# Network passes of a graph kernel: GpSimd waits for landings at every second group of gathers, and SyncE loads two groups at a time

## The chip, the cores and the metric

The kernel runs on one core of a Trainium2 chip. The metric is device time in microseconds. In this document PE is TensorE, DVE is VectorE, ACT is ScalarE, POOL is GpSimd and SP is SyncE, which computes nothing here and issues plain DMAs.

## The reference, cut to what matters

Four graph layers follow each other over 6,250 nodes of 64 features and 206,250 directed edges (sorted by destination). The change touches the third, whose message function runs twice:

```python
def _propagate(h, edge_attr, edge_index, We, be, Wl):
    x_i = h[edge_index[0]]
    x_j = h[edge_index[1]]
    x_edge = jnp.concatenate([x_i, x_j, edge_attr], axis=-1)
    x_edge = _mlp1(x_edge, We, be)              # silu(x @ W + b)
    x_edge = edge_attr @ Wl * x_edge
    x_p = _seg_mean(x_edge, edge_index[0], h.shape[0])
    return x_p + h
```

Since `We` is applied to a concatenation, the kernel adds three products: one of the node that sums (looked up from SBUF by a one-hot matmul), one of the other node (gathered from a table `q_table` in HBM), and one of the edge (stored earlier in a record of the edge, `rec_src`).

## The kernel before, in words

Edges stand in buckets of destination nodes, 128 edges to a tile, and a group is 8 tiles (`U = 8`), so 1,024 edges. There are `NG = 216` groups, and each of the two network passes (`k = 0, 1`) walks through all of them. Loops run over 54 iterations of four groups (`n = 0..3`); most buffers have four slots (`gat4`, `pay4`, `lo_bc`, `ring_i`) or two (`oht`, `msg`, `onehot`). I write g for a group's number within a pass, g = 4i + n.

The order is written out by hand on each engine, and semaphores tie the engines:

- POOL, `node_rows` and `gathers` (lines 637 to 651): for group g it waits until the 8 index columns are there (`l_idx`), then until the gathers of group g-1 have landed (`landed[(n - 1) % 4]`, which is `l_gat`), and issues 8 indirect DMAs, each of which gathers 128 rows of 64 floats into `gat4[n]`. The second wait is left out only for the first group of all.
- SP, `load_edges` (lines 521 to 523): for group g two plain loads, 552 KB of edge records into `pay4[n]` and 256 KB of digit rows, spread over the partitions, into `lo_bc[n]`. `load_all_edges` issues those of group g as soon as the message and the one-hot rows of group g-4 are done and its slots are free.
- ACT, in the order of its program for group g: `distance(g+2)` (line 862, waits for the digit rows of g+2 to land), `onehot_rows(g+1)` (line 867), `silu(g)` (line 872).
- PE, for group g: `look_up(g+1)` (line 1173, 8 matmuls, needs the one-hot rows of g+1), then `sums(g)` (line 1183, 8 matmuls, needs the message of g).
- DVE, for group g: `node_part(g)` (line 1563), `onehot_columns(g+1)` (line 1550, two operations, needs `sums(g-1)`), `edge_part(g+1)` (line 1558, waits for the gathers and the records of g+1), `message(g)` (line 1568, needs `silu(g)`), `index(g+4)` (line 1545, which lets POOL begin group g+4), and the four chained additions of `gather_sums(g-1)` (line 1578).

Line 645 is shared with a third pass of gathers, over `h_table`, which the change leaves as it is. `hold` is a wait followed by an increment of a semaphore that nothing waits for.

Of the kernel before, what the change touches and what calls it, by code (L numbers as in the profile page):

```python
# [20 lines left out]
U = 8  # L21
# [15 lines left out]
NG = TT // U  # L37
OFF = 4
# [68 lines left out]
def build(nc, a, out):  # L107
    ctx = ExitStack()
    with ctx:
# [3 lines left out]
        def sem(name):  # L113
            return ctx.enter_context(nc.semaphore(name))
# [4 lines left out]
        q_table = [nc.dram_tensor(f"q_table{k}", (NP, D), F32).ap() for k in range(2)]  # L119
# [84 lines left out]
        excess, own, first, elsewhere, trash = [dup_i[:, n] for n in range(5)]  # L204
# [39 lines left out]
        gat4 = [gat_flat[:, n * U * D:(n + 1) * U * D].rearrange("p (u d) -> p u d", u=U) for n in range(4)]  # L244
# [120 lines left out]
        l_gat = [sem(f"l_gat{n}") for n in range(4)]  # L365
# [3 lines left out]
        l_oht = sem("l_oht")  # L369
# [5 lines left out]
        l_msg = sem("l_msg")  # L375
# [35 lines left out]
        def hold(eng, s, value):  # L411

            eng.wait_ge(s, value)
            eng.sem_inc(s_passed, 1)
# [39 lines left out]
        def _(sp):  # L454
# [66 lines left out]
            def load_edges(k, i, n):  # L521
                sp.dma_start(pay4[n], rec[:, bass.ds(i * (4 * U) + n * U, U), :]).then_inc(l_pay[n], 16)
                sp.dma_start(lo_bc[n], lo_rows[bass.ds(i * 4 + n, 1), :].to_broadcast([P, U * P])).then_inc(l_lo[n], 16)

            def load_all_edges(k):
                if k:
                    sp.wait_ge(f_res, NCH * 4)
                    sp.wait_ge(l_msg, NG + OFF)
                    sp.wait_ge(l_oht, NG + OFF)
                for n in range(4):  # L530
                    load_edges(k, 0, n)
                with sp.Fori(1, NG // 4) as i:
                    for n in range(4):
                        sp.wait_ge(l_msg, i * 4 + (k * NG + n - 3 + OFF))
                        sp.wait_ge(l_oht, i * 4 + (k * NG + n - 3 + OFF))
                        load_edges(k, i, n)

            for k in range(2):
                store_table(EV_PQ + k, q_table[k], acc[:])
                load_all_edges(k)  # L540
# [29 lines left out]
        def _(pool):  # L570
# [66 lines left out]
                pool.wait_ge(d_scat[q], EI * 16 * U)  # L637


            def gathers(table, rows, landed, i, n, before, first):  # L640

                if not first:
                    hold(pool, landed[(n - 1) % len(landed)], i * (16 * U) + before)
                for u in range(U):
                    nc.gpsimd.indirect_dma_start(  # L645
                        rows[n][:, u, :], None, table,
                        bass.IndirectOffsetOnAxis(ring_i[:, n, u:u + 1], 0)).then_inc(landed[n], 16)

            def node_rows(k, i, n, first=False):
                hold(pool, l_idx, i * 4 + (k * NG + n + 1))  # L650
                gathers(q_table[k], gat4, l_gat, i, n, (k * (NG // 4) + (n > 0)) * 16 * U, first)

            for k in range(2):
                pool.wait_ge(d_table, 16 * (1 + k))
                for n in range(4):
                    node_rows(k, 0, n, first=k == 0 and n == 0)
                with pool.Fori(1, NG // 4) as i:
                    for n in range(4):
                        node_rows(k, i, n)

            def score_rows(i, n, first=False):
                hold(pool, t_idx, nth(i, n))
                gathers(h_table, gat8, t_gat, i, n, (n > 0) * 16 * U, first)
# [10 lines left out]
        def _(act):  # L674
# [104 lines left out]
            def node_copies(tr, ev, dst, rows):  # L779
                for c, (_, n) in enumerate(CHUNKS):  # L780
                    act.wait_ge(n_tr, NCH * tr + c + 1)
                    if c >= 2:
                        act.wait_ge(n_mm, NCH * ev + c - 1)
                    act.copy(dst[0:rows, c % 2, 0:n * P], bank[c % 2][0:rows, 0:n * P]).then_inc(n_cp, 1)
# [145 lines left out]
        def _(pe):  # L930
# [53 lines left out]
            def project(ev, lhs, weights, width, tr=None, chunk=None):  # L984


                if chunk:
                    chunk(0)
                for c, (_, n) in enumerate(CHUNKS):
                    if chunk:  # L990
                        if c + 1 < NCH:
                            chunk(c + 1)
                        pe.wait_ge(n_cp, NCH * tr + c + 1)
                    if c >= 2:
                        pe.wait_ge(n_ev, NCH * ev + c - 1)
                    for j in range(n):
                        b, o = bank[2 + c % 2], j * width
                        if o + width > 512:
                            b, o = bank[4 + c % 2], 0
                        last = mm(b[:, o:o + width], lhs(c, j), weights(c) if callable(weights) else weights, start=True, stop=True)  # L1000
                    last.then_inc(n_mm, 1)
# [57 lines left out]
            def project_out(k):  # L1059
                for c, (_, n) in enumerate(CHUNKS):  # L1060
                    if c % 2 == 0:
                        pe.wait_ge(a_out, (k - 1) * (DUOS + 1) + c // 2 + 1)
                    if c >= 2:
                        pe.wait_ge(n_ev, NCH * k + c - 1)
                    for j in range(n):
                        last = mm(bank[2 + c % 2][:, j * D:(j + 1) * D], out_chunk(c, j), halves(w_conv[k], c % 2), start=True, stop=True)
                    last.then_inc(n_mm, 1)
# [798 lines left out]
```

## Time and profile before

| what | value |
|---|---|
| median of 3 runs | 16204.83 us (16196.27 to 16240.02) |
| the profiled execution | 16222.93 us, span 16221.2 us |
| POOL busy | 9525.9 us (59%) |
| PE busy | 9592.5 us (59%) |
| DVE busy | 7215.4 us (44%) |
| network pass 0, gathers from first to last | 7210.7 to 10017.3 us |
| network pass 1, gathers from first to last | 10228.2 to 13035.1 us |

Busy time is the sum of the durations of an engine's instructions. A view of waits lists the idle time of an engine just before an instruction, together with what ended it; "issue" there is idle time in which the profile shows nothing that was waited for. In a timeline the number in brackets is that same idle time, and the name behind the arrow is what ended it. SPq rows are DMA issues of SP.

### The profile page before, as it was taken

To read this page: it belongs to the slowest core of one execution; us is meant where nothing else is said; L and a number is where in the kernel's file an instruction comes from. 1 tells how busy PE (TensorE), PEld (TensorE's weight loads), DVE (VectorE), ACT (ScalarE), POOL (GpSimd) and SP (SyncE) were. 2 spreads that over 40 slices of the span, in tenths; PEclk is the share of its full clock that TensorE was granted. 3 is DMA by queue.
4 is the path that set the end of the run, shared out by engine and by line. 5 is a ranking of instruction groups with operands and counts; after the bars stand their busy time and mean duration, and the time that the engine had idled before them with its cause. 6 is when DMAs were issued, how large, how long until landed. Compare 5 with 4: busy or idle time off the path is not lost.

```text
span 16221.2 us, 180153 instructions
## 1 busy us (share of the span) xinstructions
PE 9592.5 (59%) x40895; PEld 6450.1 (40%) x40896; DVE 7215.4 (44%) x18628; ACT 3844.3 (24%) x8556; POOL 9525.9 (59%) x8465
## 2 busy tenths in 40 slices
PE   0466657766478878845555556655555545555555
PEld 0111122221133333335555554555555545555554
DVE  8876657777000000013333332333333357777776
ACT  0344444442011111112222222222222212222221
POOL 0378878888645434426666664566666645555553
PEclk9999999999688778865555555555555555555555
DMA  9922222222599989992222223222222344444444
GB/s 385 358 15 19 19 15 20 20 20 18 168 342 370 343 306 357 359 113 86 84 86 84 85 84 50 75 84 86 84 86 85 80 95 139 141 141 140 140 139 96
DMA packets 1483063, 2197.01 MB, mean 135 GB/s; under 512 B 882955, under 2 KB 926027, under 8 KB 1454669
## 3 DMA queue, kind: packets, MB, share of 16 engines
q1 hardware_dynamic: 907628, 1490.52, 28.2%
q0 software_dynamic: 453120, 343.50, 12.7%
q10 hardware_dynamic: 121698, 356.43, 6.0%
q8 instruction: 184, 3.01, 0.1%
q14 instruction: 433, 3.55, 0.1%
HBM read 1771.19 MB, written 419.98 MB: 135 GB/s over the span
## 4 chain that ended last, share of the span: by engine, by line
POOL 40%; DMA 22%; issue 21%; PE 8%; DVE 4%; another core or an unknown queue 3%; ACT 1%; POOLq 0%; SPq 0%; DVEq 0%; ACTq 0%
POOL gat L645 18%; POOL adj L613 12%; POOL arena L645 8%; DMA arena<-adj 8%; DMA gat<-q_table,ring_i 6%; DMA arena<-h_table,ring_i 5%; PE bank L1029 5%; DMA adj<-put_n,put_at 2%; POOL rec_src L599 1%; DVE arena L1356 1%; PE same L1161 1%; PE same L1000 1%; DVE arena L1358 1%; PE same L980 0%
## 5 line engine op out<-in xcount | busy, mean ns | idle before, releaser
L645 POOL DMA_INDIRECT gat<-q_table,ring_i x3456 | 3626.6, 1049 | 2405.7 <-DMA gat<-q_table,ring_i 1025.0
L613 POOL DMA_INDIRECT adj<-put_n,put_at x1632 | 2559.9, 1569 | 1265.3 <-DVE put_at L1440 638.1
L1183 PE MATMUL bank<-onehot_t,onehot 128*128 128x64 f32 x6912 | 1585.5, 424 | 2574.9 <-DVE acc L1578 1880.5
L1183 PEld LDWEIGHTS bank<-onehot_t,onehot 128*128 128x128 f32 x6912 | 1506.7, 330 | 2653.8 <-DVE acc L1578 1938.5
L599 POOL DMA_INDIRECT rec_src<-pay,ring_i x1632 | 1606.4, 984 | 1566.9 <-ACTq L743 1093.2
L645 POOL DMA_INDIRECT arena<-h_table,ring_i x1728 | 1729.4, 1001 | 1346.2 <-DMA arena<-h_table,ring_i 760.8
L1088 PE MATMUL same<-onehot 32*128 32x512 f16 x3264 | 1678.6, 615 | 620.0 <-DVE onehot L1411 389.3
L1029 PE MATMUL bank<-arena,hs 128*64 128x512 f32 x5880 | 1596.0, 707 | 508.2 <-DMA arena<-adj 506.9
L1419 DVE TENSOR_SCALAR_CACHE_REDUCE onehot<-same 128x128 bf16<-128x128 f32 (+3 forms) x1632 | 1233.0, 756 | 843.2 <-PE same L1090 675.9
L1173 PE MATMUL bank<-hs,arena 128*128 x6912 | 1564.0, 421 | 29.3 <-ACT arena L867 29.3
L1173 PEld LDWEIGHTS bank<-hs,arena 128*128 128x128 f32 x6912 | 1525.9, 333 | 29.8 <-issue 29.8
L1558 DVE TENSOR_TENSOR gat<-gat,arena 128x512 f32<-128x512 f32 x432 | 299.3, 693 | 2774.6 <-DMA gat<-q_table,ring_i 2774.6
L754 ACT ACTIVATE arena<-iota_lo,arena 128x128 bf16<-128x128 f32 x3264 | 996.5, 387 | 1110.4 <-PE bank L960 926.9
L872 ACT ACTIVATE onehot_t<-gat 128x512 f32<-128x512 f32 x432 | 272.7, 631 | 3865.7 <-DVE gat L1563 3858.1
L1029 PEld LDWEIGHTS bank<-arena,hs 128*64 128x64 f32 x5880 | 525.3, 163 | 1477.0 <-issue 1473.9
L1422 DVE TENSOR_SCALAR_CACHE_REDUCE onehot<-same 128x896 bf16<-128x896 f32 (+6 forms) x1428 | 979.8, 686 | 0.0
L739 ACT COPY pay<-bank 128x260 f32<-128x260 f32 x816 | 299.9, 377 | 2283.2 <-PE bank L953 2059.2
L1509 DVE TENSOR_TENSOR acc<-bank,gat 128x512 f32<-128x512 f32 x20 | 13.8, 692 | 1828.9 <-PE bank L1038 1476.9
L1550 DVE TENSOR_TENSOR onehot<-iota_lo,keep 128x512 f32<-128x512 f32 x864 | 559.0, 689 | 566.7 <-PE bank L1183 418.2
L1239 PE MATMUL bank<-hs,pay 128*128 128x4 f32 x1728 | 386.0, 355 | 642.4 <-DVE hs L1705 478.7
L1090 PEld LDWEIGHTS same<-later,ident 128*128 128x128 f16 x1632 | 172.4, 106 | 1364.3 <-issue 1364.3
L1239 PE MATMUL bank<-hs,onehot_t 128*128 128x4 f32 x1728 | 385.2, 355 | 557.0 <-DVE hs L1705 338.3
(277 smaller groups left out, 13003.2 us busy)
## 6 DMA issues: line engine op xcount, KB each, us to landing
arena<-adj SPq DMA_DIRECT2D x300, 2560.0 KB
arena<-rec_src SPq DMA_DIRECT2D x432, 552.0 KB
adj<-hs ACTq DMA_DIRECT2D x25, 6656.0 KB, 46.3
rec_src<-pay ACTq DMA_DIRECT2D x1, 119232.0 KB, 332.0
arena<-lo_row SPq DMA_DIRECT2D x432, 256.0 KB
hs<-b_row SPq DMA_DIRECT2D x108, 1024.0 KB
acc<-b_row SPq DMA_DIRECT2D x108, 1024.0 KB
gat<-q_table,ring_i POOLq DMA_INDIRECT x3456
```

What stands on the lines that cost most here:

```text
L599: nc.gpsimd.indirect_dma_start(rec_src, bass.IndirectOffsetOnAxis(ring_i[:, q, u:u + 1], 0), pay[:, q, u, :], None, bounds_check=SLOTS - 1 ...
L613: nc.gpsimd.indirect_dma_start(counts, bass.IndirectOffsetOnAxis(put_at[:, b // 3 % 4, c:c + 1], 0), put_n[:, b // 3 % 4, c:c + 1], None, ...
L645: nc.gpsimd.indirect_dma_start(rows[n][:, u, :], None, table, bass.IndirectOffsetOnAxis(ring_i[:, n, u:u + 1], 0)).then_inc(landed[n], 16)
L754: last = act.activation(bh_lo[:, q, u, :], iota_lo[:], ACT.Abs, bias=lo_f[key][:, bass.ds(column + u, 1)], scale=-1.0)
L1029: last = [mm(sums[n], hs[:, m, :], a_ring4[(g + n) % 4][:, cell, half * ND:(half + 1) * ND], start=m == 0, stop=False) for n in range(2)]
L1088: mm(bank[2 * (n % 2) + half], rows[:, t * P:(t + 1) * P], rows[:, half * 512:(half + 1) * 512], start=True, stop=half != t // 4)
L1173: last = mm(bank[4 + n % 2][:, u * D:(u + 1) * D], oht[n % 2][:, u * P:(u + 1) * P], hs_flat[:, bass.ds(his[u // 2] * D, D)], start=True, ...
L1183: last = mm(bank[6 + n % 2][:, u // 2 * D:(u // 2 + 1) * D], onehot[:, n % 2, u, :], msg[n % 2][:, u, :], start=u % 2 == 0, stop=u % 2 == 1)
L1239: last = mm(bank[6 + (n + 1) % 2][:, u * 4:(u + 1) * 4], oht_l3[(n + 1) % 2][:, u * P:(u + 1) * P], nt[(n + 1) % 4][:, :, u // 2 + 1], sta ...
L1419: last = v.tensor_scalar(out_[:, 0:(t + 1) * P], seen[:, 0:(t + 1) * P], THR, 0.0, ALU.max, ALU.add, accum_out=s_upto[r][:, c:c + 1])
L1422: last = v.tensor_scalar(out_[:, (t + 1) * P:W * P], seen[:, (t + 1) * P:W * P], THR, 0.0, ALU.max, ALU.add, accum_out=s_past[r][:, c:c + 1])
L1550: last = v.tensor_tensor(onehot[:, n % 2, u0:u0 + U // 2], iota_lo[:].unsqueeze(1).to_broadcast([P, U // 2, P]), wide(tabs[1][:, bass.ds(i ...
```

## The change

Two places are edited. POOL's `gathers` gets a parameter `burst`, and the network passes call it with 2: the wait for the landing of group g-1 is made only where n is 0 or 2. So POOL issues the 16 gathers of a pair of groups (e and e+1, with e even) with no wait for a landing between them. The wait for the indices stays at every group, and the third pass of gathers keeps `burst=1`. SP's loop now also goes in pairs: it waits until the gathers of e-1 have landed, and until the message and one-hot rows of e-3 are done, and then issues the four loads of e and e+1 together.

```diff
                 with sp.Fori(1, NG // 4) as i:
-                    for n in range(4):
-                        sp.wait_ge(l_msg, i * 4 + (k * NG + n - 3 + OFF))
-                        sp.wait_ge(l_oht, i * 4 + (k * NG + n - 3 + OFF))
+                    for n in range(0, 4, 2):
+                        hold(sp, l_gat[(n - 1) % 4], i * (16 * U) + (k * (NG // 4) + (n > 0)) * 16 * U)
+                        hold(sp, l_msg, i * 4 + (k * NG + n - 2 + OFF))
+                        hold(sp, l_oht, i * 4 + (k * NG + n - 2 + OFF))
                         load_edges(k, i, n)
+                        load_edges(k, i, n + 1)
...
-            def gathers(table, rows, landed, i, n, before, first):
+            def gathers(table, rows, landed, i, n, before, first, burst=1):
 
-                if not first:
+                if not first and n % burst == 0:
                     hold(pool, landed[(n - 1) % len(landed)], i * (16 * U) + before)
...
             def node_rows(k, i, n, first=False):
                 hold(pool, l_idx, i * 4 + (k * NG + n + 1))
-                gathers(q_table[k], gat4, l_gat, i, n, (k * (NG // 4) + (n > 0)) * 16 * U, first)
+                gathers(q_table[k], gat4, l_gat, i, n, (k * (NG // 4) + (n > 0)) * 16 * U, first, burst=2)
```

## Rows read from the trace of the kernel before

**Rows 1.** The page: span, and the chain that ended last, by engine and line

```profile
span 16221.2 us, 180153 instructions
...
POOL 40%; DMA 22%; issue 21%; PE 8%; DVE 4%; another core or an unknown queue 3%; ACT 1%; POOLq 0%; SPq 0%; DVEq 0%; ACTq 0%
POOL gat L645 18%; POOL adj L613 12%; POOL arena L645 8%; DMA arena<-adj 8%; DMA gat<-q_table,ring_i 6%; DMA arena<-h_table,ring_i 5%; PE bank L1029 5%; DMA adj<-put_n,put_at 2%; POOL rec_src L599 1%; DVE arena L1356 1%; PE same L1161 1%; PE same L1000 1%; DVE arena L1358 1%; PE same L980 0%
```

**Rows 2.** Busy time by stretch: the two network passes (clock, DMA share, GB/s last)

```profile
7210.00:10017.00 2807.00, 1523.00 (x6880) 1483.71 (x6880) 889.85 (x2140) 588.49 (x647) 1812.93 (x1728) 0.50 0.30 83
10228.00:13035.00 2807.00, 1523.00 (x6880) 1483.69 (x6880) 889.32 (x2140) 587.54 (x646) 1813.30 (x1728) 0.50 0.30 83
```

**Rows 3.** POOL's waits, whole run: us in total, times, longest

```profile
POOL gat L645 <- DMA gat<-q_table,ring_i: 1025.0, 429, 8.4
POOL gat L645 <- issue: 961.8, 3025, 2.2
```

**Rows 4.** Timeline of one group: start, us, engine, line, operation, idle before

```profile
8041.86 0.95 POOL L645 DMA_INDIRECT gat<-q_table,ring_i  x1 [0.30 <-issue]
8044.40 0.69 DVE L1558 TENSOR_TENSOR gat<-gat,arena 128x512 f32<-128x512 f32 x1 [6.16 <-DMA gat<-q_table,ring_i]
8045.01 0.69 DVE L1568 TENSOR_TENSOR onehot_t<-onehot_t,arena 128x512 f32<-128x512 f32 x1
8045.04 1.47 POOL L645 DMA_INDIRECT gat<-q_table,ring_i  x1 [2.23 <-DMA gat<-q_table,ring_i]
...
8045.87 0.33 SPq L522 DMA_DIRECT2D arena<-rec_src  x1
...
8045.96 3.67 PE L1183 MATMUL bank<-onehot_t,onehot 128*128 128x64 f32 x16 [5.75 <-DVE acc L1578]
...
8046.39 0.33 SPq L523 DMA_DIRECT2D arena<-lo_row  x1
...
8049.43 3.62 PE L1173 MATMUL bank<-hs,arena 128*128 x16
8049.83 1.29 DVE L1550 TENSOR_TENSOR onehot<-iota_lo,keep 128x512 f32<-128x512 f32 x2 [1.07 <-PE bank L1183]
8050.57 1.37 POOL L645 DMA_INDIRECT gat<-q_table,ring_i  x1 [0.30 <-issue]
8050.74 1.15 ACT L862 ACTIVATE arena<-arena,neg_p 128x1024 bf16<-128x1024 bf16 x1 [1.24 <-issue]
8051.80 1.04 ACT L867 ACTIVATE arena<-arena 128x1024 f32<-128x1024 bf16 x1
...
8057.92 1.47 POOL L645 DMA_INDIRECT gat<-q_table,ring_i  x1 [2.23 <-DMA gat<-q_table,ring_i]
```

**Rows 5.** POOL's timeline in an earlier stage: 16 scatters in a row

```profile
4501.67 0.97 POOL L599 DMA_INDIRECT rec_src<-pay,ring_i  x1 [4.69 <-ACTq L743]
...
4511.89 0.98 POOL L599 DMA_INDIRECT rec_src<-pay,ring_i  x1 [0.30 <-issue]
...
4520.85 0.97 POOL L599 DMA_INDIRECT rec_src<-pay,ring_i  x1 [0.30 <-issue]
```

**Rows 6.** Slices of 1 us after a load was issued (DMA share, GB/s last)

```profile
8034.00:8035.00 1.00, 1.00 (x7) 1.00 (x7) 0.58 (x3) 0.00 (x0) 0.95 (x1) 0.50 0.94 212
8035.00:8036.00 1.00, 1.00 (x7) 1.00 (x6) 0.46 (x1) 0.51 (x1) 0.73 (x1) 0.50 0.99 335
8036.00:8037.00 1.00, 1.00 (x6) 1.00 (x6) 0.06 (x1) 0.12 (x1) 0.69 (x2) 0.50 0.83 309
```

**Rows 7.** Groups of instructions, 7400 to 9600 us: busy us, mean ns, idle before

```profile
L645 POOL DMA_INDIRECT gat<-q_table,ring_i x1368 | 1437.1, 1051 | 763.7 <-DMA gat<-q_table,ring_i 383.2 <-issue 380.4
...
L1558 DVE TENSOR_TENSOR gat<-gat,arena 128x512 f32<-128x512 f32 x171 | 118.5, 693 | 1064.4 <-DMA gat<-q_table,ring_i 1064.4
...
L872 ACT ACTIVATE onehot_t<-gat 128x512 f32<-128x512 f32 x171 | 108.0, 631 | 1506.1 <-DVE gat L1563 1506.1
```

## The prediction, made before the change was run

> **What bounds the kernel now.** I read the chain that ended last first, because only what lies on it can move the end. POOL carries 40% of it, and two of its lines belong to this change: the gathers of line 645 into `gat` and, as a line of its own, the transfer `gat<-q_table` that POOL waits out [rows 1]. Then I looked at the two passes as stretches of time: of 2807 us POOL is busy for 1813, PE for 1523, DVE for 890, ACT for 588, and the DMA engines are at 0.30 [rows 2]. No engine is full, so the passes are bound by an order of events. A pass of 216 groups in 2807 us is 13.0 us a group, 26.0 a pair.
>
> The view of POOL's waits says which order. In both passes POOL stood 429 times before a gather until the previous group's gathers had landed, 1025.0 us in all, 2.39 us each, and 961.8 us over 3025 times before the others, 0.318 each [rows 3]. For a group: 8 gathers of 1.051 us [rows 7] are 8.41, seven gaps of 0.318 are 2.23, one wait is 2.39, and the sum is 13.03. That is the period measured, so POOL paces the pass by itself. The timeline shows it: the last gather is issued at 8041.86 and retires at 8042.81; the landing is known at about 8044.4, when DVE starts; POOL goes on at 8045.04, and the next group begins at 8057.92, 12.88 later [rows 4]. The others wait for POOL: DVE idled 1064.4 us before 171 instances of line 1558 for gathered rows, 6.2 us each [rows 7].
>
> **The change, part by part.**
>
> *Waits removed.* Groups with n = 1 and n = 3 lose the wait: 2 in each of 54 iterations, 2 passes, 216 waits. Each costs 2.39 us of idle time now. What remains in its place is the gap between two gathers that have nothing to wait for. How large is that gap at the border of two groups, where the index wait still stands? In the stage of the scatters POOL issues two groups of 8 back to back with such a hold between them, and the gap there is 0.30 like all the others: 16 DMAs from 4501.67 to 4520.85, 1.28 apart, the ninth no later than the rest [rows 5]. So the saving is 2.39 - 0.30 = 2.09 us, times 216 = 451 us. The low bound: take the wait as it is in the calm stretch from 7400 to 9600, 383.2 / 171 = 2.24 [rows 7], and let the border cost what POOL now needs after a landing is known, 8045.04 - 8044.40 = 0.64 [rows 4]: 1.60 x 216 = 346. I take 451, since rows 5 show the border itself.
>
> Those rows also bound the other unknown, whether POOL can run 16 DMAs ahead of their landings. With no landing waited for between them, none of the 16 grew longer (0.97 to 0.98 us).
>
> *Gathers that are stretched.* A gather takes 0.95 us, but the mean is 1.051 [rows 7]: in each group two take 1.29 to 1.47. One starts at 8045.04 beside DVE's line 1568, one at 8050.57 during line 1550 [rows 4]; both operations read two SBUF operands. The loss is 0.10 x 8 = 0.8 us a group. The Trainium skill ("SBUF — State Buffer", on the shared port pair) says more: a DVE operation with two SBUF inputs and a GpSimd operation that reads SBUF exclude each other for the whole of the instruction. The rows agree in part: gathers are stretched by 0.42 to 0.52, not by a whole operation of 0.69, and a gather already under way is not stopped. Which gathers meet DVE's work shifts with the change. POOL's old pause hid most of `edge_part`, and half of the pauses go; on the other side `onehot_columns(e+1)` may now fall into the pause that is left. I take no net change, with one stretched gather a pair more or fewer as bounds: 0.42 x 216 = 91 us either way.
>
> *SP's waits and loads.* The number of loads and bytes stays. They are issued later: those of e at the landing of e-1, where today they go out at the message of e-4, beside the landing of e-3 and so 26 us sooner (those of e+1: 13 us). What is queued behind them matters. ACT needs the digit rows of e (`distance(e)`) before `onehot_rows(e-1)` and `silu(e-2)`, so PE's look-up of e-1 and DVE's message of e-2 are now late. Let t = 0 be the landing of e-1. Today the digit load is issued 0.52 us behind the record load, and ACT starts on it 8050.74 - 8046.39 = 4.35 later [rows 4]; with some 0.3 for SP to wake, the rows of e are there at 5.2. Then lines 862 and 867 (1.15 + 1.04) give 7.4, `look_up(e-1)` with 3.62 gives 11.0, `sums(e-2)` with 3.67 gives 14.7 (its message is ready at 8.7: silu 0.63 and line 1568, 0.69), `onehot_columns(e)` 16.0, `edge_part(e)` 16.7, `message(e-1)` 17.4 [rows 4, 7]. A load of one group keeps the DMA engines at 0.8 to 0.99 for about 3 us [rows 6], so the rows of e+1 come at about 8.2, before ACT asks for them. The next pair's loads need `message(e-1)` and the landing of e+1. The landing comes at 26.0 - 2.1 = 23.9, so the message is 6.5 us early and costs nothing. Without that cover each us of excess would cost 216 us. POOL needs `index(e+2)`, issued just after `message(e-2)` at about 9, at 23.9, and `index(e+3)`, at 17.6, at about 35: both are early. PE has 4 x 3.65 = 14.6 us of work in 23.9. So the delayed messages stay off the path.
>
> *Extra holds on SP* are a few instructions on an engine that idles: nothing. *Code layout:* gaps average 0.318 where the usual one is 0.30, so pauses in the issue cost 0.018 x 3025 = 54 us in all; they may double or vanish: 54 either way.
>
> **Sum.** 16222.93 (the profiled execution) - 451 = 15772. That execution lies 18 us, 0.1%, above the median of the runs shown, so the same saving from the median is 15754. I say 15765.
>
> **The rivals.**
>
> *More stretched gathers.* The exposed `edge_part` of one group in two stretches another gather each pair: 91 us if as today; 0.69 x 216 = 149 if it blocks for its whole length. For it: POOL now gathers while DVE does that work. Against it: at most one gather starts in 0.69 us. 15863 to 15921. By the rule of the skill at full strength, all of DVE's two-input work (0.69 + 0.69 + 1.29 = 2.67 us a group) would block POOL, 1.8 us more than today over 432 groups, near 800 us, and the kernel would end at about 16560; the rows speak against it, because line 1550 and line 1568 meet gathers already and cost 0.4 each.
>
> *The landings get later.* With two groups' loads (1.6 MB) started at once and 16 gathers in a row, the gathers might queue up, and POOL would meet the backlog at the pair's end. If the remaining wait grew by 1 us the time would be 15988; at 2.09 more, 4.5 us in all, the change would be worth nothing: 16223. For it: the DMA engines are full for 3 us behind a load [rows 6], 6 behind two. Against it: that is over at about 8, and the last gather is issued at 22; rows 5 show no backlog.
>
> *The loop through ACT decides* (the other side). Loads of e wait for `message(e-3)`, and that message waits for loads. The loop is 17.4 us by my walk; it must exceed 23.9 to show and 26.0 to make the kernel slower, so the digit rows would have to land at 13.8 and not at 5.2. At a loop of 28 us the passes take 2.0 x 216 = 432 us more: 16655. For it: four loads stand in one queue, and `distance` waits for a transfer already today. Against it: 8.6 us of room.
>
> *The change does nothing*: POOL's removed wait is at once replaced by another, the index wait of e+1. That would need `message(e-3)` at 10 us after the landing; it is done 6.5 us before it. 16223.
>
> **How the numbers follow.** My forecast 0.70; more stretched gathers 0.14; later landings 0.06; nothing 0.05; the loop through ACT 0.05. The likeliest one's own range is 15627 (451 + 91 + 54) to 15877 (346). The range reaches up to the worst sum of the bounds, 15877 + 91 = 15968, which takes in the second case and half of the third. Low 15620, high 15970. A measurement of this kernel tells about 0.3%, 49 us. Faster 0.91, same 0.05, slower 0.04.
>
> **What would show it.** In the profile after: POOL's waits for `gat<-q_table` fall from 429 to about 213 at 2.2 to 2.5 us each; each pass lasts 2807 - 226 = 2581 us; the gathers' mean duration stays at 1.05; PE, DVE and ACT have the same busy time. ACT starts line 862 about 5 us after a landing, and line 867 and 872 behind it. SP's four issues stand together once in 24 us and are released by a landing, not by line 1568. I would be wrong if the remaining waits are over 3 us, if gathers average over 1.1 us, or if POOL waits for line 1545 or SP for line 1568.

## The result: no gain, 0.24% slower

The changed kernel takes 16238.19 us (median of 13 runs, 16229.53 to 16261.87); the kernel before took 16203.55 us beside it (13 runs). The ratio is 1.0024, with a 95% interval of 1.0017 to 1.0031. The forecast was 15765 us, 2.7% faster.

The profile of the changed kernel spans 16241.4 us. POOL's waits come first, as they did before the change [rows 3]:

```profile
POOL gat L647 <- DVE ring_i L1547: 1471.7, 183, 210.1
POOL gat L647 <- issue: 1095.0, 3234, 3.5
...
POOL gat L647 <- DMA gat<-q_table,ring_i: 147.7, 39, 12.6
```

The waits for landings went as forecast, and further: from 1025.0 us to 147.7. In their place POOL waits for line 1547 (`index`, line 1545 before), 183 times and 1471.7 us. Before the change it did so twice, at the beginnings of the passes, for 418.9 us. The groups of instructions show a second difference:

```profile
L647 POOL DMA_INDIRECT gat<-q_table,ring_i x3456 | 3338.2, 966 | 2714.4 <-DVE ring_i L1547 1471.7
```

In the kernel before it was

```profile
L645 POOL DMA_INDIRECT gat<-q_table,ring_i x3456 | 3626.6, 1049 | 2405.7 <-DMA gat<-q_table,ring_i 1025.0 <-issue 961.8 <-DVE ring_i L1545 418.9
```

So the mean gather fell from 1.049 to 0.966 us. The four differences add up to the whole: gathers -288.4, waits for landings -877.3, "issue" +133.2, waits for indices +1052.8, sum +20.3 us. The spans differ by 16241.4 - 16221.2 = 20.2.

Why are the indices late? `index(e)` follows `message(e-4)` on DVE, so DVE lags by four groups. The view of waits, all engines, names DVE's wait. Its first row is

```profile
DVE onehot L1552 <- remote: 2464.1, 192, 16.2
```

"remote" is an end of a wait that this profile can't ascribe. The timeline of one pair shows it (start, us, engine, line, operation, idle before):

```profile
8099.25 0.94 POOL L647 DMA_INDIRECT gat<-q_table,ring_i  x1 [6.31 <-DVE ring_i L1547]
...
8101.93 3.62 PE L1175 MATMUL bank<-hs,arena 128*128 x16
8102.28 1.30 DVE L1552 TENSOR_TENSOR onehot<-iota_lo,keep 128x512 f32<-128x512 f32 x2 [1.49 <-PE bank L1185]
...
8105.10 0.33 SPq L522 DMA_DIRECT2D arena<-rec_src  x1
...
8105.34 3.62 PE L1185 MATMUL bank<-onehot_t,onehot 128*128 128x64 f32 x16
...
8106.38 0.01 SPq L523 DMA_DIRECT2D arena<-lo_row  x1
8107.20 0.69 DVE L1565 TENSOR_TENSOR gat<-gat,bank 128x512 f32<-128x512 f32 x1 [0.61 <-DVE acc L1580]
...
8107.81 0.00 SPq L522 DMA_DIRECT2D arena<-rec_src  x1
...
8109.24 0.71 SPq L523 DMA_DIRECT2D arena<-lo_row  x1
...
8112.75 3.67 PE L1175 MATMUL bank<-hs,arena 128*128 x16 [3.79 <-issue]
...
8118.46 0.94 POOL L647 DMA_INDIRECT gat<-q_table,ring_i  x1 [0.30 <-issue]
8122.20 1.29 DVE L1552 TENSOR_TENSOR onehot<-iota_lo,keep 128x512 f32<-128x512 f32 x2 [14.31 <-remote]
...
8124.01 0.69 DVE L1570 TENSOR_TENSOR onehot_t<-onehot_t,arena 128x512 f32<-128x512 f32 x1
...
8125.73 0.94 POOL L647 DMA_INDIRECT gat<-q_table,ring_i  x1 [6.32 <-DVE ring_i L1547]
```

PE's sums of line 1185 begin at 8105.34 and end, as the profile models it, at 8108.96. DVE's line 1552 needs only them, since DVE is free from 8107.89 on. It starts at 8122.20. The semaphore events of the trace agree with DVE: the increment of those sums is recorded at 8122.01, and that of the look-up after them, whose modelled end is 8116.42, at 8122.17. Two pieces of work of 3.6 us each, whose modelled ends lie 7.46 us apart, report 0.16 us apart: something held them, or their reports, up. What ends just ahead of that is POOL's stream: its last gather retires at 8119.41, 2.6 us before.

This closes a loop: a stream of 16 gathers (20.2 us), 2.6 us until the held signal is seen, then `onehot_columns`, `edge_part`, `message`, `index` and POOL's start, 3.7 us (8122.01 to 8125.73). The sum is 26.5, and the period is 26.48 (8099.25 to 8125.73). It was 26.0 before. Over both passes I matched 404 of the 432 sums with their semaphore event (the trace's record of the increment; each event goes to the latest instruction that had ended, so a delay counted this way is a lower bound). In the kernel before, where 323 could be matched, no event came over 0.02 us after the modelled end. In the changed kernel 207 came over 5 us late, 129 of them 12.5 to 13.6 us, and half of the 207 lie between 2.2 and 2.65 us behind the last gather's retirement. Only PE's reports are held: of 3562 matched increments of ACT's and DVE's instructions in these passes, 6 came over 0.02 us late.

SP is slow in the same time. Its four issues stand 1.3 to 1.4 us apart in the pair above, and 2.05 to 2.14 in another (8078.64 to 8084.97), while two neighbours stood 0.52 us apart before [rows 4].

### The profile page after: what moved, and what is told of

It reads as the page before. It is cut to its first block, busy times and chain, and to the rows that moved or that the text cites. A ratio compares the mean times of both kernels' runs of the same rounds, so it can differ in the third digit from the quotient of the medians.

```text
span 16241.4 us, 180149 instructions
## 1 busy us (share of the span) xinstructions
PE 9591.9 (59%) x40895; PEld 6449.7 (40%) x40896; DVE 7191.6 (44%) x18628; ACT 3811.1 (23%) x8556; POOL 9236.8 (57%) x8465
## 4 chain that ended last, share of the span: by engine, by line
POOL 23%; another core or an unknown queue 18%; issue 17%; DMA 16%; PE 13%; DVE 8%; DVEq 3%; ACT 1%; SPq 0%; POOLq 0%; ACTq 0%
POOL adj L615 12%; POOL arena L647 8%; DMA arena<-adj 8%; DMA arena<-h_table,ring_i 5%; PE bank L1031 5%; PE bank L1185 4%; DMA adj<-put_n,put_at 2%; DVE onehot_t L1570 1%; POOL rec_src L601 1%; DVE arena L1358 1%; PE bank L1175 1%; DVEq L1580 1%; DVE onehot L1552 1%; DVE acc L1580 1%
## 5 line engine op out<-in xcount | busy, mean ns | idle before, releaser
L647 POOL DMA_INDIRECT gat<-q_table,ring_i x3456 | 3338.2, 966 | 2714.4 <-DVE ring_i L1547 1471.7
L1175 PE MATMUL bank<-hs,arena 128*128 x6912 | 1597.3, 420 | 1033.2 <-issue 896.2
L864 ACT ACTIVATE arena<-arena,neg_p 128x1024 bf16<-128x1024 bf16 x432 | 495.4, 1147 | 2153.7 <-DMA arena<-lo_row 1879.0
```

The lines of the kernel that those rows point to most:

```text
L647: nc.gpsimd.indirect_dma_start(rows[n][:, u, :], None, table, bass.IndirectOffsetOnAxis(ring_i[:, n, u:u + 1], 0)).then_inc(landed[n], 16)
L1175: last = mm(bank[4 + n % 2][:, u * D:(u + 1) * D], oht[n % 2][:, u * P:(u + 1) * P], hs_flat[:, bass.ds(his[u // 2] * D, D)], start=True, ...
```

## The experiments

Two theories at first. **A**: POOL's unbroken stream of gathers is what holds the signals up. **B**: the late burst of four loads does.

### Each half of the change alone

```diff
 # pool_only against the changed kernel: SP as before
-                    for n in range(0, 4, 2):
...
+                    for n in range(4):
+                        sp.wait_ge(l_msg, i * 4 + (k * NG + n - 3 + OFF))
+                        sp.wait_ge(l_oht, i * 4 + (k * NG + n - 3 + OFF))
                         load_edges(k, i, n)
-                        load_edges(k, i, n + 1)
...
 # sp_only against the changed kernel: POOL as before
-gathers(q_table[k], gat4, l_gat, i, n, ..., first, burst=2)
+gathers(q_table[k], gat4, l_gat, i, n, ..., first)
```

> POOL's half of the change alone: it waits for a landing at every second group, while SP issues the loads of g at the message of g-4 as before. Theory A (the gather stream): as soon as POOL issues 16 gathers without a pause, what PE has finished is seen by DVE and ACT only when POOL's stream ends (in the changed kernel 13 us late, 2.6 us behind the last gather). Then this kernel is as slow as the changed one, 16200 to 16300, and POOL waits for line 1547 at the pairs' starts. Theory B (the loads): the late burst of four loads is what stalls; then this kernel gets the predicted gain, about 15770.

Measured: 16224.31 us (10 runs, 16094.88 to 16318.1), ratio 0.9996 [0.9971, 1.0021]. The waits of POOL:

```profile
POOL gat L645 <- DVE ring_i L1545: 1352.3, 163, 214.1
POOL gat L645 <- issue: 1156.3, 3252, 3.3
...
POOL gat L645 <- DMA gat<-q_table,ring_i: 152.8, 41, 12.6
```

They are like those of the changed kernel, and A stands: POOL's half loses its own gain without any help from SP's. The mean gather takes 0.963 us here, so gathers get shorter without SP's half too. The stall isn't equally strong everywhere: the times of this kernel scatter by 1.4%, and in its profile pass 0 lasts 2728.1 us and pass 1 2854.7 (2806.6 and 2806.9 before). Over much of pass 0 pairs take about 22 and 27 us in turn, 24.5 in the mean. Why this second rhythm arises isn't known.

> SP's half alone: loads in pairs, at the landing of e-1, while POOL waits at every group as before. Theory A: every stream has 8 gathers and a pause of 2.4 us behind it, so nothing stalls: 16150 to 16250. Theory B: the burst of four loads stalls the engines, some 13 us at each pair minus what is hidden: over 16600.

Measured: 15990.12 us, ratio 0.9852 [0.9836, 0.9868]. B is refuted, but A's 16150 to 16250 is missed too: **SP's half alone is a gain of 1.5%.** Its waits and its gathers:

```profile
POOL gat L647 <- issue: 1113.0, 3086, 2.4
...
POOL gat L647 <- DMA gat<-q_table,ring_i: 911.9, 366, 9.5
...
POOL gat L647 <- DVE ring_i L1547: 395.7, 4, 203.3
```

```profile
L647 POOL DMA_INDIRECT gat<-q_table,ring_i x3456 | 3365.2, 974 | 2420.6 <-issue 1113.0
```

Against the kernel before: gathers -261.4 us, waits and "issue" +14.9 (1113.0 + 911.9 + 395.7 against 961.8 + 1025.0 + 418.9), sum -246.5. The spans differ by 237.6. So the gain lies in the gathers, whose mean falls from 1.049 to 0.974 us. By place in the group, the first gather of each group takes 158.8 us less in all and the fifth 137.0 less, and the other six 34.4 more. The timeline shows where the late loads put DVE's work:

```profile
8074.55 1.33 DVE L1552 TENSOR_TENSOR onehot<-iota_lo,keep 128x512 f32<-128x512 f32 x2 [4.06 <-remote]
...
8075.15 0.94 POOL L647 DMA_INDIRECT gat<-q_table,ring_i  x1 [2.25 <-DMA gat<-q_table,ring_i]
...
8075.80 0.68 DVE L1560 TENSOR_TENSOR gat<-gat,arena 128x512 f32<-128x512 f32 x1
...
8080.06 1.15 ACT L864 ACTIVATE arena<-arena,neg_p 128x1024 bf16<-128x1024 bf16 x1 [16.80 <-DMA arena<-lo_row]
...
8082.71 0.69 DVE L1570 TENSOR_TENSOR onehot_t<-onehot_t,arena 128x512 f32<-128x512 f32 x1 [6.23 <-issue]
```

ACT now waits for the digit rows, so `message` (line 1570) comes some 7 us after `edge_part` and no longer beside POOL's first gather behind a landing. That gather took 1.47 us before [rows 4] and takes 0.94 here. This is the delay through ACT that the prediction walked through, to half a microsecond: the last increment of the landing is recorded at 8074.38, so line 864 starts 5.7 us behind it, where I had 5.2. The fifth gather is spared because `onehot_columns` (line 1552) has moved to the landing.

Whether a gather is stretched follows from one thing, counted over all gathers: whether it begins while DVE runs an operation on two SBUF operands. It then ends as if it had begun 0.56 us into that operation, within 0.04 us for all 860 such gathers of the kernel before and for 489 of 577 here; the other 88 began within 0.04 us of the operation and took 0.94, as if they had come first. Begun 0.1 us into it, a gather takes 1.40 us here; 0.3 into it, 1.21; 0.6 into it, 0.94. A gather already under way when such an operation begins takes 0.94 to 0.95 in both kernels. The 860 gathers of the kernel before (428 in line 1568, 432 in line 1550) cost 358 us in all; the 577 here cost 104, since most begin late in the operation.

"Nothing stalls" in theory A was wrong too. DVE's line 1552 in the timeline had waited 4.06 us for sums whose modelled end is 8071.81 and whose increment is recorded at 8074.39, with POOL pausing behind every 8 gathers. Of 350 matched sums 200 report over 1.2 us late, at most 3.99, and half of the 200 come more than 1.6 us behind the last gather. The place in the stream tells which: all 135 that end within 5 us of the stream's first gather report at once, and 200 of the 202 that end over 7 us into it are late. In the kernel before every matched sum but four, which lie outside a stream, ends within 5 us of the first gather. So a stream of 8 is enough for the delay; the pause behind it ends the delay before POOL needs the indices, which it waits for only 4 times.

### POOL never pauses

```diff
 # two_behind against the kernel before, in node_rows; first is now true for the first two groups
-                gathers(q_table[k], gat4, l_gat, i, n, (k * (NG // 4) + (n > 0)) * 16 * U, first)
+                if not first:
+                    hold(pool, l_gat[(n - 2) % 4], i * (16 * U) + (k * (NG // 4) + (n > 1)) * 16 * U)
+                gathers(q_table[k], gat4, l_gat, i, n, 0, True)
```

> POOL waits at every group, but for the landing of g-2 and not g-1, so that it never pauses; SP as before. Theory A: the stream has no end until POOL runs out of indices (4 groups, 40 us), DVE waits that long for PE, and the time is 16200 or more. Theory B: 432 waits of 2.1 us are gone, 900 us, and the time is about 15300 to 15400.

Measured: 16293.32 us in one run (16235.54 before). Waits for landings are 1.2 us in all, and those for indices

```profile
POOL gat L645 <- DVE ring_i L1547: 1817.7, 229, 221.9
```

A again: 1023.8 us of landings gone, 1398.8 us of indices come.

### The loads' volume

```diff
 # small_loads2: inside the loop, for both groups of a pair
-                        load_edges(k, i, n)
+                        load_first_tiles(k, i, n)   # pay4[n][:, 0:1] and lo_bc[n][:, 0:P]
```

> The changed kernel in which SP's loads inside the loop bring only the first of 8 tiles of each group (69 KB of records and 32 KB of digit rows instead of 552 and 256); the other 7 tiles are computed from what the first four groups left in the slots. Theory A (the gather stream alone stalls): the loads' volume doesn't matter, 16150 to 16300, with DVE waiting for PE until POOL's stream ends. Theory B (stream and load traffic together): no stall, and the removed waits show: 15450 to 15800.

Measured: 16135.34 us in one run (16192.4 before). What it computes is wrong, since seven of eight tiles hold old records, but it has as many gathers and matmuls as the changed kernel. In the stretch from 7400 to 9600 us the DMA share is 0.12 in place of 0.29:

```profile
7400.00:9600.00 2200.00, 1239.45 (x5508) 1201.80 (x5508) 702.92 (x1717) 453.74 (x516) 1322.98 (x1374) 0.50 0.12 29
```

and DVE waits on:

```profile
DVE onehot L1556 <- remote: 2055.0, 187, 16.5
```

The time is 0.4% below the kernel before and 0.6% below the changed kernel's 16238.19, by a single run. So the stall stays with 0.12 in place of 0.29 of DMA traffic; a kernel without any loads wasn't run.

### A pause in the middle of the pair, without a landing

```diff
 # in node_rows, ahead of the index wait; 512 f32 columns (pause_short) or 2048 bf16 (pause_long)
+                if n % 2:
...                      # a hold for the memset before
+                    nc.gpsimd.memset(idle[:], 0.0).then_inc(s_idle, 1)
```

> The changed kernel with a memset of 128x512 on POOL (about 0.5 us) between the two groups of a pair, with no wait for a landing. Theory A1 (the stalled signals of PE come through only when the gathers in flight have drained, so a pause must be about as long as a landing, 1.4 us): still as slow as the changed kernel, 16200 to 16300. Theory A2 (any gap in POOL's gathers lets them through): the index waits go, and the time is about 15600 (the changed kernel's passes at 16 x 1.25 + 0.5 + 2.3 = 22.8 us a pair).

> The same with a memset of 128x2048 (some 1.8 us) in place of the removed wait: again no landing is waited for in the middle of a pair. Theories A1 and A2: with a pause as long as a landing the signals come through, POOL waits for indices no longer, and the time is that of SP's half alone, 15900 to 16000. If what counts is the semaphore wait for the landing itself and not the pause: 16300 or more (the changed kernel plus up to 390).

Measured: pause_short 16233.04 us in one run (16192.4 before), with the memset at 0.545 us and POOL's waits still

```profile
POOL gat L649 <- DVE ring_i L1553: 1138.3, 136, 218.1
```

pause_long 15898.05 us in one run (16192.4 before); its memset takes 1.825 us, and the waits for indices are 417.0 us in 6 times, about what the passes' beginnings cost before (418.9). With more runs:

> The kernel with a POOL memset of 1.8 us in the middle of each pair, timed in rounds: 15880 to 15960, ratio 0.979 to 0.984; the landing that it doesn't wait for is not needed.

Measured: 15983.25 us beside 16278.1, ratio 0.9814 [0.9798, 0.983]. The ratio is inside what I expected, the time just above, as is that of the kernel before. So nobody needs the landing in the middle of a pair; what the removed wait gave was a pause of about 2 us. Half a microsecond is too short. A2 is refuted and A1 fits. That the landings themselves release PE's reports isn't shown: the late ones come a median 0.3 us behind the last recorded landing here and 1.4 us behind it in the changed kernel, and many landings are missing from the traces.

### Slower gathers

```diff
 # paced: 128 columns; paced_1col: 1 column
                 for u in range(U):
...                      # a hold for the memset before
+                    nc.gpsimd.memset(idle[:], 0.0).then_inc(s_idle, 1)
                     nc.gpsimd.indirect_dma_start(
```

> The changed kernel with a memset of 128x128 (0.2 us) before every gather, so that gathers follow each other in about 1.45 to 1.5 us in place of 1.25. Theory that the rate of gathers counts: nothing stalls, POOL sets the pace, 16 x 1.5 + 2.3 = 26.3 us a pair: about 16280, with waits for landings and not for indices. Theory that an unbroken stream counts whatever its rate: the stall lasts as long as the stream, 24 + 2.6 + 3.7 = 30.3 us a pair: about 17000.

> As the paced run (15887, gathers every 1.34 us), but the memset before each gather covers one column (about 0.1 us) and may hide in the gap there is. Theory R (the rate of gathers counts): at a pitch near 1.25 us the stall is back, POOL waits for indices, 16150 to 16300. Theory M (another instruction of POOL between two gathers is enough): no stall, 16 x 1.25 + 2.3 = 22.3 us a pair, about 15500 to 15600.

Measured: paced 15886.67 us in one run (16192.4 before). A gather comes every 1.34 us there and not every 1.25:

```profile
8001.29 0.95 POOL L653 DMA_INDIRECT gat<-q_table,ring_i  x1 [0.17 <-issue]
8002.24 0.22 POOL L652 MEMSET idle<- 128x128 f32 x1
8002.63 0.95 POOL L653 DMA_INDIRECT gat<-q_table,ring_i  x1 [0.17 <-issue]
```

I expected a pitch of 1.5, hence the missed figure. paced_1col, with the memset hidden in the gap and the pitch at 1.25, takes 16409.67 us in one run (16247.83 before), above my 16150 to 16300, and waits for indices 179 times, 1465.3 us. So an instruction between the gathers doesn't help; 0.09 us per gather does. With more runs:

> The paced kernel again, timed in rounds: 15880 to 15900, ratio to the kernel before 0.979 to 0.983.

Measured: 15940.92 us beside 16247.83, ratio 0.981 [0.9794, 0.9826]. The ratio is as expected, the time 40 us above.

> The paced gathers in bursts of two groups, with SP's loads as in the kernel before. Tells what the late loads are worth once nothing stalls. If they matter only by moving DVE's two-input operations away from the starts of gathers: the gathers' mean duration is back near 1.05 (0.06 us x 3456 = 200 us more than the paced run), about 16090. If they don't matter when gathers are paced: 15890.

Measured: 15970.57 us in one run (16247.83 before), 30 us or 0.2% above the paced kernel's 15940.92 beside the same kernel before, which a single run can't tell from nothing. The gathers' mean is 1.003 us against 0.998 there (0.990 in the first paced run), not the 1.05 that I expected. So with paced gathers SP's late loads are worth little or nothing.

```diff
 # paced_two_behind: paced, SP as before
+                    hold(pool, l_gat[(n - 2) % 4], ...)   # in node_rows, in place of the landing of g-1 at even n
```

> The paced gathers with POOL waiting for the landing of g-2, so that it never stops for a landing, and SP's loads as before. Theory R: at 1.34 us a gather nothing stalls however long the stream is; 8 x 1.38 = 11.0 us a group against 12.1 in the paced run: about 15400. If the length of the stream counts at this rate too: POOL waits for indices, 15900 or more.

Measured: 16331.05 us, ratio 1.0054 [1.0037, 1.0071].

```profile
POOL idle L650 <- DVE ring_i L1553: 1314.9, 177, 216.9
```

At the slower pitch a stream with no end stalls too. Pitch alone is not the condition: in the paced kernel the signals of the sums are also late, by 6.3 us (median of the 211 over 1.2 us) and not 13, and released 1.8 us behind the last gather. The smaller number isn't the pitch's doing by itself: the late sums end mostly 16.5 to 18 us into the stream there and 9 to 10.5 in the changed kernel, so less of the stream is left. What differs is the look-up: 160 of its 373 late signals come through while the stream still runs, against 24 of 209 in the changed kernel. POOL then waits for indices only at the passes' beginnings (427.0 us, twice).

### Streams of 12

```diff
-                if not first and n % burst == 0:
+                if not first and (burst == 1 or n in (0, 3)):
...
+                    if burst == 2 and n == 1 and u == 4:
+                        hold(pool, landed[1], i * (16 * U) + (own + 16 * 4))
```

> The changed kernel with POOL waiting for a landing before gathers 0, 12 and 24 of each 32: streams of 12, 12 and 8 gathers (15 and 10 us long) and three pauses in four groups instead of two. If the stall sets in only towards the end of 16 gathers: nothing waits for PE, and against SP's half alone (15990) 108 more waits of 2.1 us are gone: 15765. If it sets in 7 us into a stream, as the late SP issues and signals of PE suggest: the gain shrinks or turns over, 15950 to 16200, with waits for indices back.

Measured: 15960.07 us beside 16278.1, ratio 0.9806 [0.979, 0.9823]. That is 0.46% below SP's half alone by the ratios, 75 us where 227 were to be had:

```profile
POOL gat L649 <- DVE ring_i L1550: 552.3, 37, 210.8
```

Of 403 matched sums 227 report over 1.2 us late, a share like that in SP's half alone, but 129 of them over 5 us, where SP's half alone has none. The longer stream holds them longer, and that takes part of the gain.

## Why the prediction was wrong

**The bound and the arithmetic of the waits** were right. POOL paced the passes, and the landing waits fell by 877.3 us, more than the 451 forecast, since by then POOL was mostly late for another reason: 39 landing waits are left, not about 213, and 183 waits for `index`, which the prediction had named as a sign of being wrong.

**The step that failed** is the one that bounded "whether POOL can run 16 DMAs ahead of their landings" by [rows 5]. They show that POOL's own DMAs don't grow longer, and that held: the gathers after the change take 0.94 to 0.95 us, 0.30 apart, in a row of 16, but for those that begin beside DVE's work. They don't show what a row of 16 does to the others. I took the pause behind each group for lost time, while it also bounded how long a signal of PE can be held: with a pause behind 8 gathers the sums' signals are at most 3.99 us late (sp_only), with 16 in a row mostly 13. The removed 216 waits came back as waits for `index`, 1052.8 us more than before. pool_only (0.9996) and two_behind show it without SP's half, pause_short (one run) shows that 0.545 us don't help, and pause_long shows that a pause of 1.8 us undoes it.

**The walk through ACT** was right up to the signals. In sp_only ACT starts 5.7 us behind the landing, where I had 5.2. For the changed kernel the walk took PE's results to be known as they end (`sums` 14.7, `onehot_columns` 16.0) and so put `message(e-1)` 6.5 us ahead of need; it comes behind the stream's end. The rival "the change does nothing" gave the right time, 16223, and named the right wait in kind, the index wait. Its mechanism was the index of e+1, 10 us into a pair; the wait that came is that of e, at the pair's start. I gave it 0.05.

**The stretched gathers** were put at no net change, 91 us either way. They went down by 288.4 us in the changed kernel and 261.4 in sp_only. This term has the right mechanism and was mis-sized: the bound counted one gather a pair where about three changed (288.4 / 216 = 1.34 us a pair; 849 gathers took over 1.2 us before, 150 after). SP's half moves the operations as shown above. In the changed kernel it isn't needed for this: pool_only has 0.963 us a gather without it, and in the pair shown DVE does its two-input work from 8122.20 to 8124.70, while POOL stands waiting for the index. The rule of the Trainium skill ("SBUF — State Buffer", Who interferes with whom) is that a DVE operation with two SBUF inputs and a GpSimd instruction that reads SBUF contend, and that the loser is fully blocked. The traces agree: a gather that begins inside such an operation loses what is left of the operation's first 0.56 us, up to 0.53. I had read the 0.42 to 0.52 us as less than the rule says, but the gathers had begun a little into the operation. The 16560 that I put down for the rule's full strength took every such operation to block POOL for its whole length, which fits only a gather that is ready to start when the operation does.

The Trainium skill ("SBUF — State Buffer", SBUF: two separate sides) says of the engines' side that PE, ACT and DVE's own ports "never wait on anyone". That is about ports; the measured delay of 13 us in PE's signals beside a stream of gathers isn't covered by it, and no run here shows that SBUF ports are its cause.

**What stays open** is the mechanism. Shown are its conditions. PE's reports are late when its work ends late in a stream of gathers, over 7 us behind the first one at a pitch of 1.25 us. A stream of 8 is enough for 1.4 to 4 us. They come through mostly 1.6 to 2.6 us behind the last gather, so the delay grows with what is left of the stream: 13 us with 16 gathers. A pause of 1.8 us ends it, one of 0.5 us doesn't. It needs neither SP's late burst nor more than 0.12 of DMA traffic. Place in the stream isn't all: the look-ups of the kernel before end 7 to 8 us behind the first gather and report at most 1.04 us late, most of them at once. Whether PE's matmuls themselves or only their reports are held isn't told by the profile, since matmul ends are modelled. A variation of the gathers' bytes wasn't tried.

## What to carry to other kernels

A wait in a steady loop can be a pause that other engines live on. Before removing one, ask not only what the waiting engine does with the time but what the others get done in it, and after removing it look for signals that arrive behind their instruction's end. When an edit has two halves, time each alone: here SP's half alone gains 1.5%, which POOL's half hid, and the better versions (16 gathers with a 1.8 us pause or paced at 1.34 us, streams of 12) stand at 0.981 of the kernel before.

## What the runs showed of the hardware that I had not expected

- With 16 gathers in a row at 1.25 us, increments of PE's matmuls were recorded 13 us behind the modelled end, and SP's DMA issues stood 1.3 to 2.1 us apart instead of 0.52. ACT's and DVE's increments were not late. With streams of 8, sums that ended over 7 us into one were still 1.4 to 4 us late.
- 0.09 us more per gather (1.34 against 1.25) let part of PE's signals through while the stream ran and made the kernel 2% faster than the kernel before; a pause of 0.545 us in the middle did nothing, one of 1.825 us did.
- A gather that begins inside a DVE operation on two SBUF operands ends as if it had begun 0.56 us into it, so it takes up to 0.53 us longer; one already under way isn't stretched. In the kernel before this cost 358 us over 3456 gathers.
